# Causal mask of the narrow heads' transposed scores: a GpSimd select on the exponentials in place of TensorE products of mask and identity

## What is computed

```python
def _L1_attn_ref(x, Wq, Wk, Wv, Wo):
    H = N_HEADS            # 16
    hd = D // H            # 8
    q = (x @ Wq.T).reshape(B, S, H, hd).transpose(0, 2, 1, 3)
    k = ...; v = ...
    scores = jnp.einsum('bhcd,bhsd->bhcs', qi, k) * scale
    mask = kpos[None, :] <= qpos[:, None]
    scores = jnp.where(mask, scores, jnp.finfo(scores.dtype).min)
    p = jax.nn.softmax(scores, axis=-1)
    return (None, jnp.einsum('bhcs,bhsd->bhcd', p, v))
    ...
    return out @ Wo.T

x = x + _L0_attn_ref(xn, ...) + _L0_ffn_ref(xn, ...)
xn = _layernorm(x, axis=-1)
x = x + _L1_attn_ref(xn, ...) + _L1_ffn_ref(xn, ...)
```

## Time and profile before

| | |
|---|---|
| runs, median of 3 | 4898.7 us (4894.94 to 4906.26) |
| the profiled execution | 4894.27 us |
| its span, first to last instruction | 4892.5 us |
| busy in the span: PE, PEld, DVE, ACT, POOL | 92%, 53%, 67%, 56%, 45% |
| mean granted TensorE clock | 0.976 |
| products of mask and identity on the transposed scores (L737) | 512 |
| exponentials of the transposed scores (L860) | 512 |

### The profile page before, as it was taken

How to read it: one execution, slowest core, us unless ns; L and a number is a source line. 1 busy time by engine, 2 the same in 40 slices (tenths; PEclk the granted TensorE clock), 3 DMA queues, 4 the chain that set the end, 5 groups by cost and what they waited for, 6 DMA issues and landing times. The chain is left out here.

```text
span 4892.5 us, 175691 instructions
## 1 busy us (share of the span) xinstructions
PE 4513.9 (92%) x67980; PEld 2599.0 (53%) x67980; DVE 3266.0 (67%) x5738; ACT 2741.6 (56%) x5520; POOL 2215.4 (45%) x2020
## 2 busy tenths in 40 slices
PE   7888888888869999999999999999999999999995
PEld 4445445444435555555555555555555555555553
DVE  4544544545537777777777777777777777777773
ACT  3434434433425666566666666666666666666663
POOL 0000000000017666766666666666676666666661
PEclk9999999999989999999999999999999999999997
DMA  1000000000002111221112111221112111221112
GB/s 36 8 6 8 4 6 8 4 6 8 4 19 60 45 46 46 62 53 42 49 47 68 41 51 45 58 54 46 45 45 67 46 45 45 60 53 49 46 47 61
DMA packets 144809, 188.61 MB, mean 39 GB/s; under 512 B 34151, under 2 KB 66170, under 8 KB 144138
## 3 DMA queue, kind: packets, MB, share of 16 engines
q1 hardware_dynamic: 144138, 178.32, 13.5%
HBM read 29.32 MB, written 4.19 MB: 7 GB/s over the span
## 5 line engine op out<-in xcount | busy, mean ns | idle before, releaser
L1312 POOL TENSOR_TENSOR cs<-cs 128x512 f32<-128x512 f32 x768 | 980.3, 1277 | 569.0 <-DVE cs L1623 564.0
L1439 PE MATMUL psum<-wqkv,xw 128*128 128x512 f32 x2304 | 1192.5, 609 | 31.8 <-POOL xw L1349 24.9
L1623 DVE TENSOR_TENSOR cs<-psum,rots 128x1024 f32<-128x1024 f32 x768 | 938.4, 1222 | 293.3 <-PE psum L1439 260.5
L1321 POOL TENSOR_TENSOR qk<-cs,rn 128x512 f32<-128x512 f32 x768 | 777.2, 1044 | 338.1 <-ACT rn L1505 283.8
L1521 ACT ACTIVATE sq<-psum 128x512 f32<-128x512 f32 x768 | 459.3, 598 | 654.4 <-DVE cs L1623 625.9
L1347 POOL MEMSET qTl<- 128x2048 f32 x1 | 1.8, 1805 | 1433.7 <-POOLq L497 1433.7
L1584 DVE TENSOR_REDUCE ss<-sq 128x8 f32<-128x512 f32 x768 | 520.3, 677 | 7.0
L1390 PEld LDWEIGHTS psum<-pT,vw 64*64 64x64 f32 x18624 | 399.9, 135 | 190.2 <-issue 190.0
L1444 PEld LDWEIGHTS psum<-ident,qk 128*128 128x128 f32 x3088 | 352.8, 141 | 265.4 <-issue 154.5
L1444 PE MATMUL psum<-ident,qk 128*128 128x128 f32 x3088 | 445.9, 278 | 48.4 <-DVE state L1657 31.4
L1439 PEld LDWEIGHTS psum<-wqkv,xw 128*128 128x128 f32 x2304 | 368.6, 190 | 196.0 <-issue 171.2
(11 more groups left out here) (201 smaller groups left out, 7081.1 us busy)
## 6 DMA issues: line engine op xcount, KB each, us to landing
vw<-vl SPq DMA_DIRECT2D x768, 128.0 KB, 2.4
vw<-vl SPq DMA_DIRECT2D x672, 64.0 KB, 2.0
wqkv<-in_wqkv SPq DMA_DIRECT2D x42, 256.0 KB, 3.5
wol<-in_wol SPq DMA_DIRECT2D x7, 512.0 KB, 4.3
w1l<-in_w1l SPq DMA_DIRECT2D x7, 341.0 KB
xin<-in_x SPq DMA_DIRECT2D x9, 256.0 KB, 2.8
xr<-in_x SPq DMA_DIRECT2D x8, 256.0 KB, 4.0
sums<-sumout SPq DMA_DIRECT2D x8, 256.0 KB, 2.3
```

The costliest lines, as they stand in the source:

```text
L1312: summed_rot.done(nc.gpsimd.tensor_tensor(own, own, halves(cs[:, t % 2, j, 1, :])[:, :, ::-1, :], ALU.add), at)
L1321: rotated.done(nc.gpsimd.tensor_tensor(qk[:, j, :].rearrange("p (h c) -> p h c", c=EL), cs[:, t % 2, j, 0, :].rearrange("p (h c) -> p h c" ...
L1439: last = nc.tensor.matmul(ps[:, :], xw[:, t * P:(t + 1) * P], wqkv[:, col:col + BANK], start=True, stop=True)
L1623: parts.done(V.tensor_tensor(cs[:, t % 2, j, :, :].rearrange("p i (h c) -> p i h c", c=EL), twice, by_head, ALU.mult), at)
```

## The change

The four mask products of every `("bt", r, j)` go. The first pass's scores are now started and ended by one product each, which itself counts up the semaphore that ACT waits for. ACT takes the exponential of the unmasked scores. A new loop on POOL waits for the last of the four exponentials of a key, and then sets, with one `affine_select` over the first 128 columns of all four heads (128 partitions x 4 x 128), those entries to zero in which the query precedes the key. PE's wait before `("bp", r, j)` is now for this select (semaphore `cut`) in place of the exponentials. The `("bs", r, i)` keys keep their mask products. The semaphores `passed` of the passes become one; nothing waits for it.

```diff
@@ mixed_layer
-    link, rlink, passed = sem("link"), sem("rlink"), buf.passed
+    cut = steps("cut", lambda key: ("bp", *key[1:]) if key[0] == "bt" else None)
+    link, rlink, passed = sem("link"), sem("rlink"), sh.passed
@@ block.gpsimd
+            cut.prime(pool)
+
+            def body(it, s):
+                for key in order:
+                    if key[0] == "bt":
+                        j = key[2]
+                        pool.wait_ge(exped_b.sem, exped_b.value(it, (key[1:], RANKS - 1)))
+                        settle(pool, passed)
+                        own = pb[:, j % 2, :, 0:P]
+                        cut.done(nc.gpsimd.affine_select(own, own, [[0, RANKS], [1, P]], ALU.is_ge, zero, 0, -1), ("bp", *key[1:]))
+
             if not opening:
+                if cut.keys:
+                    zero = nc.gpsimd.to_reg(0.0)
+                    each_trip(pool, body)
                 return
@@ block.tensor, "bt"
                     for g in range(RANKS):
                         rows = slice(32 * g, 32 * g + 32)
-                        nc.tensor.matmul(banks[g][:, 0:N - j * P], kz1[rows, r, j * P:(j + 1) * P], qz1[rows, r, j * P:N],
-                                         start=True, stop=False)
-                    for g in range(RANKS):
-                        ring.steps.done(nc.tensor.matmul(banks[g][:, 0:P], maskc[:, :], identb[:, :],
-                                                         start=False, stop=True), (*key, g))
+                        ring.steps.done(nc.tensor.matmul(banks[g][:, 0:N - j * P], kz1[rows, r, j * P:(j + 1) * P],
+                                                         qz1[rows, r, j * P:N], start=True, stop=True), (*key, g))
@@ block.tensor, "bp"
-                    pe.wait_ge(exped_b.sem, exped_b.value(it, (at, RANKS - 1)))
+                    pe.wait_ge(cut.sem, cut.value(it, key))
                     settle(pe, passed)
```

More of the change, by code:

```diff
@@ L217, in __init__ @@
         self.lnt = sb("lnt", [P, 1])
+        self.passed = ctx.enter_context(nc.semaphore("passed"))
         self.state = sb("state", [P, B + 1, N + 1])
@@ L345, in __init__ @@
         self.oT1, self.sumout = sb("oT1", [P, N]), sb("sumout", [P, T, D])
-        self.const_loaded, self.const_made, self.passed = (ctx.enter_context(nc.semaphore(n)) for n in
-                                                             ("const_loaded", "const_made", "passed0"))
+        self.const_loaded, self.const_made = (ctx.enter_context(nc.semaphore(n)) for n in ("const_loaded", "const_made"))
 def pass0(nc, io, sh, ctx):
@@ L1175, in transformer @@
     gelued = steps("gelued", lambda key: key[1] if key[0] == "gate" else None)
-    link, rlink, passed = sem("linkl"), sem("rlinkl"), sem("passedl")
+    link, rlink, passed = sem("linkl"), sem("rlinkl"), sh.passed
     def readers(key):
@@ L1686, in pass2 @@
     xf, sums, out = sb("xf", [P, N]), sb("sums_in", [P, T, D]), sb("outs", [P, T, D])
-    straight, turned, added, loaded, stored, passed = (sem(n) for n in ("straight", "turned", "added", "loaded",
-                                                                         "stored2", "passed2"))
+    straight, turned, added, loaded, stored = (sem(n) for n in ("straight", "turned", "added", "loaded", "stored2"))
+    passed = sh.passed
     tokens = "s (t p) d -> p (s t) d"
```

## The result

| | before | changed |
|---|---|---|
| median of 4 runs | 4897.8 us (4894.9 to 4906.3) | 4930.4 us (4927.6 to 4933.8) |
| ratio, 95% interval | | 1.0063 (1.0051 to 1.0076) |
| profiled execution, span | 4894.3, 4892.5 us | 4927.6, 4925.9 us |
| mean granted clock of the span | 0.976 | 0.966 |

What follows compares the result with a forecast made beforehand. The prediction took a chain passing from engine to engine in the narrow attention as the bound. Ranks 0 to 2 cost 0.45 us, rank 3 1.80: 2.25 per sequence, times 8 = 18, so 4898.7 + 18 = 4917 us; range 4896 to 4950.

Steps and rivals of the forecast that it cites:

- the 18 us of the sum: Narrow attention: 0.45 us for ranks 0 to 2 plus 1.80 for rank 3, 2.25 us longer per sequence, times 8.
- the chain: Work passing from engine to engine in the narrow attention, said to set its length; forecast 2.25 us longer per sequence.
- The select: POOL's new operation per key in the narrow attention, over 512 elements per partition: taken as 1.0 us.
- The hand-overs: Around POOL's new operation: ACT to POOL taken as 0.15 us, POOL to PE as 0.14 us.
- The chain for a given select: Narrow attention's length worked out for POOL times of 0.61, 1.0 and 1.28 us: 1, 18 and 38 us longer in total.
- rank 3: Last rank of a narrow attention, no next scores in between: last product forecast 1.80 us later, 0.83 with 0.61 us.
- ranks 0 to 2: First three ranks of a narrow attention: each forecast 0.15 us longer, or 0.24 shorter with 0.61 us for POOL.
- That a shift of the last product is a shift of the program: PE queue after a rank's last product: any delay of that product was taken to delay the whole program equally.
- the first stretch: A narrow attention before the change, 64.0 us at granted clock 1.00, PE busy 52.4: cited against clock loss.
- The rival: Clock falls more often in the narrow attentions: 10 us on top (4927) or 28 us (4945); chance 0.13.

Runs made afterwards that it cites:

- the filled kernel: The kernel before the change, with 106 unused 128x128 bf16 zero-matrix products per sequence in front of PE's longest waits: 4852.6 us, ratio 0.9915.

## Why the prediction was right and wrong

The time, 4930.4 us, lies in the range of 4896 to 4950, and slower was forecast with 0.70. But the 18 us of the sum were for the wrong reason: the chain costs 2 to 3 us and not 18, and the clock, at nothing in the sum, costs 30. That two errors of opposite sign ended inside the range is in good part luck; the range had room for some loss of clock, the forecast of 4917 had none.

*The select, "I hold it nearest to the product with a broadcast operand and take 1.0 us"*: **this step failed**. It takes 0.634. The row to hold it to was the copy's 0.61: beside it the position, the comparison and the choice add no more than 0.02 us. The rule of the Trainium skill that was cited ("GPSIMD Engine Reference", section "Performance pitfalls for Q7 kernels") allows this only by its unrolled figure: 1.03 cycles give an estimate of 0.44 us and leave 0.19, which no run here takes apart, while 2.03 give 0.87, more than was measured.

*The hand-overs*, 0.15 and 0.14: measured 0.16 and 0.14.

*The chain for a given select*: right. For 0.61 us the prediction gave a rank 0.24 us shorter and rank 3 0.83 longer; measured 0.22 and 0.88 at 0.634. That in ranks 0 to 2 the fourth product has the one long wait, and that in rank 3 the first, the third and the fourth are late, is as the working had it for a select of 1.0 us, too; the 0.3 us that it then had before the third product of ranks 0 to 2 did not come with the shorter select.

*That a shift of the last product is a shift of the program*: right for the change. The part behind the last narrow attention took 3449.3 and 3449.7 us.

*The clock, "Against it: in the first stretch PE waited in the same places, and the clock stayed"*: this is where the real cost was argued away. The rival had a chance of 0.13 and a price of 10 to 28 us; measured, it is 30 us, nearly the whole result. The one stretch at 1.00 was weak evidence: it is the only one of the eight attentions of that trace without a stretch at half clock. What its text named as the cause, products taken out and waits put in, fits the totals as a pair, which I had not seen: the four combinations of products and select gave 0, 0, 6 and 30 us for the clock, where the 6 is 21 in the one profile. The Trainium skill's warning about gaps ("TensorE: Matmul & The Clock Gate", section "Why this matters for your kernels") points the right way, but the gaps that it names are longer than any within the narrow attention, where PE idles 1.3 us at most in the kernel before and 1.4 in the changed one, and the clock falls all the same; the measurement decides.

## What to carry to other kernels

Before taking products from a TensorE that waits for other engines, look at the granted clock of the stretch in several trips: if it falls in some of them, idle time has a price beyond the chain, and the sum must hold it. Products of zero into an idle accumulator, in front of PE's longest waits, cost nothing where they end inside the wait, and here bought 0.85%. And when an operation moves to an engine with slack, move only those instances whose hand-over the chain hides; here nine of sixteen gained 15 us, and 20 on top of the filled kernel, while all sixteen cost 32.5.

## What was not expected of the hardware

A select over 4 x 128 f32 elements per partition costs GpSimd 0.634 us, a copy of 513 costs 0.614, so the comparison adds 0.02 us at most. Two selects in a row are spaced 0.58 us.

Products of a zero matrix keep the clock up as others do: 106 per sequence raised the granted clock of the first part from 0.95 to 0.99.

Longer waits cost more clock: twice the select took the clock's part from 30 to 66 us. But the waits do not seem to be all of it, since the changed kernel's waits with the mask products beside them had 6 us by the totals. In which of its attentions a kernel falls, and for how long, differs within one execution, so one profile alone doesn't price it; the medians are the better guide. What exactly decides a fall was not tried.
